# x of the first batch multiplied ahead of its edge features for four chunks, with earlier W1, reordered gathers and a last chunk by tiles

## The reference

```python
h = jnp.maximum(_layernorm(x, axis=-1), 0.0)
out1 = segment_sum(edge_attr, col, n)                 # sum of a node's edges
out2 = where(cnt > 0, segment_max(edge_attr, col, n), 0)
out3 = out1 / maximum(cnt, 1)
h2 = concatenate([h, out1, out2, out3, u[batch]], axis=1)   # batch is 0 everywhere
y = relu(h2 @ W1 + b1) @ W2 + b2
return x + y + h
```

## Time and profile before

| | us |
|---|---|
| median of 3 runs | 550.93 (550.51 to 552.75) |
| the profiled execution | 551.13 |
| its span | 549.3 |
| PE / DVE / ACT / POOL busy | 498.4 / 437.6 / 391.6 / 247.6 |
| first product of layer 1 | 54.64 |
| last product / first scatter issued | 537.03 / 538.55 |

### The profile page before, as it was taken

How to read it: one execution, slowest core, us unless ns; L and a number is a source line. 1 busy time by engine, 2 the same in 40 slices (tenths; PEclk the granted TensorE clock), 3 DMA queues, 4 the chain that set the end, 5 groups by cost and what they waited for, 6 DMA issues and landing times.

```text
span 549.3 us, 9292 instructions
## 1 busy us (share of the span) xinstructions
PE 498.4 (91%) x3182; PEld 454.8 (83%) x3182; DVE 437.6 (80%) x766; ACT 391.6 (71%) x1136; POOL 247.6 (45%) x260
## 2 busy tenths in 40 slices
PE   0494999989999999998999999999999999999991
PEld 0253998879999999987988888888888888889990
DVE  4828886999898999989899898988988987539420
ACT  1655788888787979977787787786967785574430
POOL 2343434456355574848457367174372560300211
PEclk9998899999999999998999999999999999999997
DMA  2972443354445363654644356255253340100100
GB/s 102 286 276 84 123 127 105 104 196 143 158 124 198 98 220 104 189 200 158 198 136 153 119 172 189 82 180 178 72 185 126 120 147 8 39 1 1 39 20 19
DMA packets 18838, 71.14 MB, mean 130 GB/s; under 512 B 4571, under 2 KB 5755, under 8 KB 18776
## 3 DMA queue, kind: packets, MB, share of 16 engines
q0 software_dynamic: 15408, 65.72, 36.8%
q1 hardware_dynamic: 3378, 4.79, 2.8%
HBM read 64.09 MB, written 6.85 MB: 129 GB/s over the span
## 4 chain that ended last, share of the span: by engine, by line
PE 75%; DVE 13%; ACT 3%; issue 3%; another core or an unknown queue 2%; DMA 2%; POOL 0%; DVEq 0%; POOLq 0%; ACTq 0%
PE l1ps L687 30%; PE l1ps L691 15%; PE yps L705 14%; PE yps L709 7%; PE l1ps L694 4%; PE tps L672 3%; DVE work L911 2%; DVE work L900 2%; DVE work L922 1%; PE tpr L675 1%; DMA work<-in_dst 1%; DVE hl L1000 1%; DMA xr<-dstp,rowi 1%; ACT work L495 1%
## 5 line engine op out<-in xcount | busy, mean ns | idle before, releaser
L362 POOL DMA_INDIRECT work<-in_edge_attr,idx x98 | 124.4, 1269 | 169.8 <-DVE work L922 97.1
L504 ACT ACTIVATE hff<-l1ps,b1e 128x512 f32<-128x512 f32 (+2 forms) x128 | 74.7, 584 | 101.4 <-PE l1ps L694 98.3
L687 PE MATMUL l1ps<-inh,w1h 128*128 128x512 f32 (+2 forms) x512 | 117.9, 352 | 5.2 <-issue 1.9
L495 ACT ACTIVATE work<-work,mk 128x96 f32<-128x96 f32 x411 | 116.0, 370 | 0.0
L691 PE MATMUL l1ps<-inl,w1h 128*128 128x512 f32 (+2 forms) x512 | 113.5, 344 | 0.9 <-DVE inl L1004 0.9
L687 PE MATMUL l1ps<-inh,w1l 128*128 128x512 f32 (+2 forms) x512 | 113.7, 344 | 0.0
L911 DVE TENSOR_TENSOR work<-work 128x192 f32<-128x192 f32 (+9 forms) x154 | 110.3, 738 | 1.1
L1000 DVE TENSOR_TENSOR hl<-hff,hh 128x512 fp32r<-128x512 f32 (+2 forms) x128 | 72.0, 567 | 47.3 <-ACT hh L506 32.7
L381 POOL DMA_INDIRECT out_y<-xr,oidx x49 | 68.1, 1391 | 88.7 <-DVE xr L1031 74.0
L705 PE MATMUL yps<-w2h,hh 128*128 128x256 f32 x392 | 99.6, 284 | 0.0
L705 PE MATMUL yps<-w2l,hh 128*128 128x256 f32 x392 | 98.2, 280 | 0.0
(11 more groups left out here) (162 smaller groups left out, 558.5 us busy)
## 6 DMA issues: line engine op xcount, KB each, us to landing
work<-in_L_gnn_W SPq DMA_DIRECT2D x2, 1024.0 KB, 6.2
work<-in_edge_attr,idx POOLq DMA_INDIRECT x98
xr<-in_L_gnn_W SPq DMA_DIRECT2D x1, 1024.0 KB
xr<-in_x,nid POOLq DMA_INDIRECT x49
out_y<-xr,oidx POOLq DMA_INDIRECT x49
work<-in_dst SPq DMA_DIRECT2D x1, 415.0 KB
dstp<-in_dst SPq DMA_DIRECT2D x1, 415.0 KB
hff<-in_L_gnn_W SPq DMA_DIRECT2D x3, 128.0 KB
```

Source lines behind the costliest of these rows:

```text
L362: pool.indirect_dma_start(out=runs[:, j * k * F:(j + 1) * k * F], out_offset=None, in_=edge, in_offset=bass.IndirectOffsetOnAxis(ap=idx[:, ...
L495: last = act.activation(es[g % 2][:, at * F:(at + 1) * F], run2(g)[:, at * F:(at + 1) * F], ACT.Copy, scale=mk[:, a + j, e:e + 1])
L504: act.activation(hf[C % 2][:, 0:cols], l1ps[C % 2][:, 0:cols], ACT.Relu, bias=b1e[:, m:m + 1])
L687: pe.matmul(ps, wt[:, c, ks(m)], inh[b % 2][:, c, 0:cols], start=(c == 0 and wt is w1h), stop=False)
```

## The change

- The table `dstp` has rows of 85 numbers instead of 50 (window 1105 instead of 1050, 10 comparisons instead of 17). It is written from `sd` after `sd` has landed, instead of from `dst` at once; W1's first half is loaded right behind it, and the `seam` load behind that.
- ACT widens W1's first half before the window instead of after the search.
- POOL gathers `run2`, `run1` and x of group 0 after the third `idx_ready`, then waits for the flag, then gathers group 1.
- x of batch 0 is transposed by itself as soon as it is normalized (`x_transposes`), copied out in one piece, and its products for chunks 0 to 3 (24 of the 52 of these chunks) are done before the edge features are transposed. Chunks 2 and 3 use `yps` 1 and 3. DVE's `x_in_lo` stands between two levels of group 0's tree.
- The masks of group 1 are made by DVE alone, in `tree_head`; ACT's half is gone, and with it the semaphore `own_path`. Warm-up products: 8 instead of 20.
- The last batch keeps its two tiles in separate PSUM banks; the last chunk's products are ordered by tile, and DVE adds and POOL scatters each tile when it is done.

The core of the diff:

```diff
-    WARM = 20
+    WARM = 8
     def width(b):
...
-    STEP = 50
+    STEP = 85
     SPR = SC // STEP
     NS = NE // STEP
+    assert KC == 4 and D == 2 * P
     assert SR * SC == NE and SR <= P and SPR * STEP == SC and NS * STEP == NE
-    WIN = 21 * STEP
+    WIN = 13 * STEP
...
+        return yps[b % 2 * 2 + (j if b == NB - 1 else j // 2)]
+    def yplace(b, j):
+        at = 0 if b == NB - 1 else j % 2 * D
+        return ybank(b, j)[:, at:at + D]
...
             sp.dma_start(sd[0:SR, 0:SC], dst_sd).then_inc(sd_in, 16)
             sp.wait_ge(seam_free, 2)
-            sp.dma_start(dstp[0:NS, :], dst.rearrange("(r c) -> r c", c=STEP)).then_inc(dstp_in, 16)
             sp.dma_start(dstp[NS:NS + WIN // STEP, :], tail[:, :]).then_inc(dstp_in, 16)
+            sp.wait_ge(sd_in, 16)
+            sp.dma_start(dstp[0:NS, :].rearrange("(r s) c -> r (s c)", s=SPR), sd[0:SR, 0:SC]).then_inc(dstp_in, 16)
+            sp.dma_start(raw1[0], W1[0:2 * P, :].rearrange("(c p) h -> p c h", p=P)).then_inc(w1a_in, 16)
             sp.dma_start(sd[0:SR - 1, SC:SC + 1], dst_sd[1:SR, 0:1], allow_slow_non_contiguous=True).then_inc(seam_in, 16)
             sp.wait_ge(win_in, 16)
-            for c in range(0, KC, 2):
-                sp.dma_start(raw1[c // 2], W1[c * P:(c + 2) * P, :].rearrange("(c p) h -> p c h", p=P)).then_inc((w1a_in, w1b_in)[c // 2], 16)
+            sp.dma_start(raw1[1], W1[2 * P:4 * P, :].rearrange("(c p) h -> p c h", p=P)).then_inc(w1b_in, 16)
             for r in range(3):
                 sp.dma_start(raw1r[r * KR:(r + 1) * KR, :], W1[KC * P:K, :]).then_inc(w1r_in, 16)
...
                                             bounds_check=N - 1, oob_is_err=False).then_inc(stored[b % XS], 16)
-            pool.wait_ge(idx_ready, 1)
-            gather_x(0, [0])
-            pool.wait_ge(idx_ready, 2)
-            gather_run1(0)
             pool.wait_ge(idx_ready, 3)
             gather_run2(0)
-            gather_x(0, list(range(1, width(0))))
-            pool.wait_ge(low_ps, W1A_LOWS)
-            gather_run2(1)
-            gather_run1(1)
-            gather_x(1, list(range(width(1))))
+            gather_run1(0)
+            gather_x(0, list(range(width(0))))
             pool.wait_ge(flag_ready, 1)
             general = pool.value_load(flag[0:1, 0:1], min_val=0, max_val=1)
...
             gather_general(0)
+            pool.wait_ge(low_ps, W1A_LOWS)
+            gather_run2(1)
+            gather_run1(1)
+            gather_x(1, list(range(width(1))))
             for s in range(-1, NB + 1):
...
             act.activation(warm[:, 0:1], pid[:, :], ACT.Sqrt)
             act.wait_ge(ident_ready, 1)
             act.activation(negid[:, :], ident[:, :], ACT.Copy, scale=-1.0).then_inc(ident_ready, 1)
+            act.wait_ge(w1a_in, 16)
+            act.activation(w1h[:, 0:2, :], raw1[0], ACT.Copy).then_inc(w_hi, 1)
             act.wait_ge(thr_ready, 1)
             act.wait_ge(win_in, 16)
             act.activation(dwf[0][:, 0:WIN], dw[:, :], ACT.Copy).then_inc(widened, 1)
...
                     act.wait_ge(l1_done, (b - 1) * HC)
                 act.activation(inh[b % 2][:, :, ks(k)], trans_bank(b, k)[:, :].rearrange("p (c n) -> p c n", n=P), ACT.Copy).then_inc(hiT_done, 1)
+            def x_in_hi():
+                act.wait_ge(xt_done, 1)
+                act.activation(inh[0][:, 0:2, 0:2 * P], tps[:, :].rearrange("p (c n) -> p c n", c=2), ACT.Copy).then_inc(xhi_done, 1)
+            def edges_in_hi(k):
+                act.wait_ge(trans_done, k + 1)
+                act.activation(inh[0][:, 2:4, ks(k)], trans_bank(0, k)[:, 2 * P:4 * P].rearrange("p (c n) -> p c n", n=P), ACT.Copy).then_inc(hiT_done, 1)
             def rem_in_hi(b):
                 n = width(b)
                 act.wait_ge(trans_done, t_of[b][-1] + 1)
...
             low_parts(10, len(LOWS))
-            mask(1, 0, 2)
             norm(0, 0)
             norm(0, 1)
+            x_in_hi()
             means(0)
-            in_high(0, 0)
-            in_high(0, 1)
+            edges_in_hi(0)
+            edges_in_hi(1)
+            rem_in_hi(0)
             sums(1)
             act.wait_ge(bias_set, 1)
...
+            def x_transposes():
+                for k in range(2):
+                    pe.wait_ge(h_done, k + 1)
+                    for c in range(2):
+                        last = pe.transpose(xfirst(c)[:, ks(k)], cat[:, place(0, k), ks(c)], ident[:, :])
+                last.then_inc(xt_done, 1)
+            def x_products():
+                cols = width(0) * P
+                pe.wait_ge(xhi_done, 1)
+                for m in range(XFIRST):
+                    for wt in (w1h, w1l):
+                        for c in range(2):
+                            pe.matmul(l1bank(m)[:, 0:cols], wt[:, c, ks(m)], inh[0][:, c, 0:cols], start=(c == 0 and wt is w1h), stop=False, skip_group_check=True)
+                pe.wait_ge(xlo_done, 1)
+                for m in range(XFIRST):
+                    for c in range(2):
+                        pe.matmul(l1bank(m)[:, 0:cols], w1h[:, c, ks(m)], inl[0][:, c, 0:cols], start=False, stop=False, skip_group_check=True)
             def transposes(b, k):
                 t = t_of[b][k]
                 g = next(g for g in g_of[b] if groups[g][5] <= t < groups[g][5] + groups[g][1])
                 pe.wait_ge(over_done, g + 1)
                 pe.wait_ge(h_done, t + 1)
                 pe.wait_ge(outs_done, t + 1)
-                if t >= 2 or trans_bank(b, k) is tps and t:
+                if t >= 2:
                     pe.wait_ge(loT_done, t if trans_bank(b, k) is tps else t_of[b][0])
-                for c in range(KC):
+                for c in range(0 if b else 2, KC):
                     pe.transpose(trans_bank(b, k)[:, ks(c)], cat[:, place(b, k), ks(c)], ident[:, :])
                 if k == 0 and b:
                     pe.wait_ge(rem_lo, b)
...
                     pe.wait_ge(hiT_done, t_of[b][-1] + 1)
                 if C >= 2:
                     pe.wait_ge(hi_done, C - 1)
-                ps = l1ps[C % 2][:, 0:cols]
+                ps = l1bank(C)[:, 0:cols]
+                parts = range(2 if C < XFIRST else 0, KC)
                 for wt in (w1h, w1l):
-                    for c in range(KC):
-                        pe.matmul(ps, wt[:, c, ks(m)], inh[b % 2][:, c, 0:cols], start=(c == 0 and wt is w1h), stop=False)
+                    for c in parts:
+                        pe.matmul(ps, wt[:, c, ks(m)], inh[b % 2][:, c, 0:cols], start=(c == 0 and wt is w1h), stop=False, skip_group_check=C < XFIRST)
                 if m == 0:
                     pe.wait_ge(loT_done, t_of[b][-1] + 1)
-                for c in range(KC):
-                    pe.matmul(ps, w1h[:, c, ks(m)], inl[b % 2][:, c, 0:cols], start=False, stop=False)
+                for c in parts:
...
             for _ in range(WARM):
                 pe.matmul(yps[3][:, 0:2 * P], w1h[:, 0, 0:P], w1h[:, 1, 0:2 * P], start=True, stop=True)
             pe.wait_ge(low_out, len(LOWS))
+            x_transposes()
+            x_products()
             transposes(0, 0)
             transposes(0, 1)
             for C in range(NCH):
...
                 for k in range(width(s + 1) if s + 1 < NB else 0):
                     if trans_at(s + 1, k) == m:
                         transposes(s + 1, k)
-            for C in range(NCH - 2, NCH):
-                layer2(C)
+            def last_layer2(C):
+                pe.wait_ge(hi_done, C + 1)
+                for j in range(width(NB - 1)):
+                    y = yplace(NB - 1, j)
+                    for wt in (w2h, w2l):
+                        pe.matmul(y, hh[C % 3][:, ks(j)], wt[:, HC - 1, :], start=False, stop=False, skip_group_check=True)
+                    if j == 0:
+                        pe.wait_ge(lo_done, C + 1)
+                    pe.matmul(y, hl[C % 3][:, ks(j)], w2h[:, HC - 1, :], start=False, stop=True, skip_group_check=True).then_inc(last_done, 1)
+            layer2(NCH - 2)
+            last_layer2(NCH - 1)
         @block.vector
         def _(dve):
...
             def tree_head(g):
                 a, n, k1, k2, _, _ = groups[g]
                 s = es[g % 2]
+                if g < 2:
+                    masks(g)
+                else:
+                    dve.wait_ge(masked, g - 1)
                 dve.wait_ge(run1_in[g % 2], run_count(g))
-                if g == 0:
-                    masks(0, 0, n)
-                else:
-                    dve.wait_ge(masked, g)
...
+            def x_in_lo():
+                dve.wait_ge(xhi_done, 1)
+                V.tensor_tensor(out=inl[0][:, 0:2, 0:2 * P], in0=tps[:, :].rearrange("p (c n) -> p c n", c=2), in1=inh[0][:, 0:2, 0:2 * P], op=ALU.subtract).then_inc(xlo_done, 1)
+            def edges_in_lo(k):
+                dve.wait_ge(hiT_done, k + 1)
```

(15 more changed lines are left out.)

54 lines of the change are left out of this document (27 added, 27 removed).

## The result

The changed kernel took **549.32 us** (median of 16 runs, 545.46 to 550.66) where the kernel before took 550.74 beside it (16 runs, 548.97 to 553.17): ratio 0.9959, 95% interval 0.9943 to 0.9975. The forecast was 546.1, a gain of 4.9 us; 1.4 to 2.3 us are there. Its profiled execution took 545.46 us (span 543.7, against 549.3), which is the fastest of the 16; most lie near 549.3. Both facts need an explanation, and the second turned out to lead to the first.

What follows compares the result with a forecast made beforehand. The prediction took PE to bound the body, DVE close behind, and the change to touch only start and end. From 551.13 it took 4.4 us at batch 1 and 0.65 at the end: 546.1 us, range 543.0 to 552.6.

Steps and rivals of the forecast that it cites:

- DVE's stall at the check: DVE's 7.47 us wait for PE's check matmul goes in thinner traffic; DVE goes on at 33.8 instead of 38.81, -5.0 us.
- The end: Last chunk done tile by tile: both scatters start 0.65 us earlier.
- DVE is idle ahead of `x_in_lo`: A new wait in DVE's queue for batch 0's x, idle from 45.4 to 46.4, then busy 0.69 us.
- PE's clock falls in the front: PE's clock was expected to fall to 1.2 GHz around x's products and be back near 52.
- The index chain: Start of the kernel: copying `dstp` out of `sd` makes the search later, between 0.5 us earlier and 3.1 later, taken as +2.5.
- where ACT and PE are also through with their low parts: ACT and PE finish low parts at 42 to 43.6 as today, so DVE's scales for `norm` at 43.9 find them ready.
- From there nothing changes: After batch 1's start PE, DVE and POOL move together, so the 4.4 us gained there last through the body.
- x ahead: Batch 0: 24 products go where PE idles; chunk 0 done at 54.5 (low clock) or 52.3 (full) instead of 57.8.
- That sum (-4.4): Batch 1, worked out from DVE's first sum of group 1, starts 3.6 or 5.4 us early; -4.4 taken.
- Clock and window at their ends: Rival: other clock and index-chain cases, 543.1 or 546.9, window held longer by W1 550.0; forecast with variants (543 to 548) 0.63.
- the stall comes back: Rival: PE's report is held as long as gathers run, whatever their density; 552.0 us, chance 0.14.
- The slower case: Rival: search 5.5 us late and the stall as today, check seen at 42.8; about 555 us, chance 0.09.

Runs made afterwards that it cites:

- e4: The kernel before with one edit, POOL issues group 1's six gathers after the flag instead of ahead of it: 545.81 us, ratio 0.9895 to the kernel before.
- e11: The kernel before with group 1's gathers behind the flag, repeated on another chip: 545.31 us, ratio 0.9888 to the kernel before.
- e7: The changed kernel with group 1's six gathers put back ahead of POOL's wait for the flag: 547.77 us, ratio 1.0109 to the kernel before.
- e5: The changed kernel with PE running remainder products 8 and 9 ahead of the check's matmul of `bad`: 545.47 us, ratio 1.0073 to the kernel before.
- e14: The changed kernel with remainder products 8 and 9 ahead of the matmul of `bad`: 545.10 us, against 549.11 for the changed kernel on the same chip.
- e2: The changed kernel without multiplying x of batch 0 ahead: 548.58 us, ratio 0.9952 to the kernel before.
- e10: The changed kernel, unchanged, run again on another chip with its own profile: 550.24 us, ratio 0.9966 to the kernel before.
- e9: The kernel before, unchanged, with its own profile: 552.38 us, ratio 1.0008 to the kernel before beside it.
- e3: The changed kernel with group 1's masks moved on DVE to just ahead of `x_in_lo`: 547.46 us, ratio 0.9933 to the kernel before.
- e8: The changed kernel with the old index chain and group 1's masks ahead of `x_in_lo`: 540.45 us, ratio 0.9981 to the kernel before.
- e13: The changed kernel, unchanged, run once more on another chip: 549.11 us, ratio 1.0135 to the kernel before, which took 541.37 there.
- e15: The changed kernel with remainder products 8 and 9 ahead of the matmul of `bad` and 28 warm-up products instead of 8: 543.69 us, ratio 1.0042.
- e18: The kernel before with group 1's gathers behind the flag, on a further chip: 543.37 us, ratio 0.9887 to the kernel before.

## Why the prediction was wrong

**Right.** DVE's stall at the check goes, and it is worth more than anything else in this kernel. The end gave 0.5 of 0.65. DVE is idle ahead of `x_in_lo`, and PE's clock falls in the front. The point on which the stall was decided, gathers into full traffic at the check, held as well: the forecast counted ten in a row (the trace has twelve, from 21.65 to 35.42), e4 and e11 isolate the four edge gathers and two of x that are group 1's, and e7 speaks for the thinner traffic.

**The index chain: +4.5 instead of +2.5.** The term was mis-sized by its first row. I took 5.50 us for the copy as an *upper* bound, from the load of the same shape; it measured 7.28 (7.31 in e5, 7.25 in e7). The single packets of 3400 B took 0.219 us each in the mean, against 0.162 in the load; the first starts at 7.13 and the last ends at 13.28. Whether the direction does that was argued and not shown: W1's first half, which the change queues right behind, has its first packet at 7.76. The copy's packets take 0.23 us in the mean before that, 0.24 from 8 to 11 us with W1's beside them, and 0.16 to 0.18 from 11 to 13, where few of W1's are. No run has the copy alone. Either way a row with another direction and nothing beside it was no upper bound. The rule of the Trainium skill that I weighed, "DMA: Bandwidth & Descriptors", section "Why a DMA increments its semaphore by 16 and not by 1", would have 5 engines for 125 rows; the trace agrees as far as it shows, with mostly five packets of the copy under way at once. It spoke against this edit; I took its consequence into the sum, priced by the load. The other half of the term, W1 on ACT and the seam test on DVE ahead of the window, cost nothing: both were done when it came. DVE went on at 34.97 instead of 33.8: of the 5.0 us of the stall's term, 3.8 were left.

**The step that failed** is the half sentence "where ACT and PE are also through with their low parts (as today, at 42 to 43.6)". Nothing in the kernel before made PE wait for `bad`: the sum stood in its list where it had come by late. The change makes W1's first half early, so PE is through with its eight first remainders at about 31, and makes `bad` late by the 4.5 us of the index chain. Between the two PE stands 3.5 to 3.75 us in front of work that is ready. I asked who waits for the moved steps on SP, POOL, DVE and ACT, and not on PE, the engine that the profile names as the bound. The price is not only the wait but the low clock after it: in the kernel before the last remainders were done by 42 to 43.6, here at 46.8 in one execution and 49 in others, so `norm`'s start went from 48.93 to 47.35 or 49.79 where I had 43.9. e14 measured the step by itself: 4.0 us in the median, 2.4 of them at chunk 0, in executions whose clock stays low. That the forecast's 546.1 and these 4.0 add up to the 549.1 to 550.2 that were measured is luck in part: without the step e14 is 2.3 us ahead of the kernel before at batch 1 where the forecast had 4.4, and 2.7 more arise between 200 and 275 us, where it had "From there nothing changes".

**x ahead.** I had chunk 0 at 54.5 or 52.3; it came at 55.2 and 57.7. That is a follower of the step above. But e2 shows that even so it carries nothing further than chunk 0: the forecast's sum had not rested on it, since batch 1 was worked out from DVE's first sum of group 1. That sum (-4.4) failed because `norm` was 3.5 to 5.9 us late, through DVE's wait of 3.4 to 5.8 us where I had 1.0: -2.1 was measured in the first profile and -1.0 in e10 against e9. In addition the forecast put the masks ahead of a free DVE; e3 (1.7 us in the front) and e8 (1.6 in the median) show what was to be had by another place, which I had not seen.

**The rivals.** "Clock and window at their ends" had 550.0 for a window held 3.1 us longer, by another mechanism; "the stall comes back" (552.0) did not occur in any profile of the changed kernel. The slower case needed both the late chain and the stall; it did not occur either. The change was slower than the kernel before in one group (e13), by 7.7 us. No rival held that what it takes away may not be there, and that this is the reason is a reading. All my rows of before came from one execution, and I took the stall in it as always there. The measured time lies in the range (543.0 to 552.6), but on the far side of its middle.

## To carry to other kernels

When a change makes one operand of a queue's next step earlier and another later, look at that engine's list for the step that needs the late one, and put work that is ready in front of it; on PE the standing can cost most by the clock after it. Try the smallest part of a change alone: here one moved group of gathers gave 6.4 us, and the whole change on the same chip 1.5. Price a transfer by a row of the same direction and with the same traffic beside it, and if there is none, call the nearest row a guess and not a bound.

## What the runs showed of the hardware

- A copy of 125 rows of 3400 B from SBUF to HBM took 7.28 us, the load of the same shape 5.61 in the same execution; packets 0.219 against 0.162 us. The copy had W1's first half beside it from 7.76 on and the load had not, so direction and company are not told apart.
- PE's clock fell in or right behind 3.5 to 3.75 us of standing and stayed at 0.50 for up to 12 us with PE busy nearly all the while (e10, e13), or came back to 0.94 and 0.91 from 38 to 42 and fell again (the first profile): same program, nearly the same waits, 2.4 us apart at batch 1. In e15 it fell after two waits of 0.58 and 0.78 us, in e14 not after 1.06.
- From PE's start of the sum of `bad` to DVE's copy of it 6.5 us passed in the first profile of the kernel before, with DVE waiting 7.5 to 8.1 us in all three profiles of it, and 0.5 us in the changed kernel. In the kernel before, group 1's gathers make the difference (e4, e11, e18). Neither full traffic without gathers (e11, 0.23 us at 411 GB/s) nor gathers in falling traffic (e7, 0.47 us) held the report.
- The kernel before took 541.4 us in two groups of runs and 550 to 552 in the other four; the changed kernel took 549 to 550 in all three where it ran. Each of the experiments' groups had a chip of its own.
